# A tile of tokens takes one position of each quarter of 32 images, and x is loaded once

## The reference

```python
x = x + _L0_conv_ref(_gn(x), ...)      # group norm over (rows, columns, 2 channels), window attention + 3x3 convolution
t = _to_tokens(x)                      # (32, 256, 64)
t = t + _L1_attn_ref(_ln_t(t), ...)    # scores are sums over all 256 positions; softmax over the 32 images
t = t + _L1_ffn_ref(_ln_t(t), ...)     # top 2 of 8 experts, hidden size 682
return _from_tokens(t, x)
```

## Time and profile before

| what | us |
|---|---|
| median of 3 runs | 887.52 |
| profiled execution | 889.28 |
| its span | 887.4 |
| TensorE busy | 787.4 |
| VectorE busy | 623.4 |
| ScalarE busy | 436.9 |
| GpSimd busy | 395.0 |
| reload of x, median of its four DMAs from issue to landing | 7.7 |

### The profile page before, as it was taken

The page is one execution under the profiler, slowest core; times in us unless marked ns, Lnnn a source line. Parts: engine busy times, 40 slices in busy tenths (PEclk is TensorE's granted clock), DMA queues, the critical chain, the costliest instruction groups (busy, mean ns, idle before and its releaser), DMA issues.

```text
span 887.4 us, 22282 instructions
## 1 busy us (share of the span) xinstructions
PE 787.4 (89%) x7948; PEld 476.6 (54%) x7948; DVE 623.4 (70%) x1522; ACT 436.9 (49%) x828; POOL 395.0 (45%) x452
## 2 busy tenths in 40 slices
PE   4789999999978999799898879689989999999970
PEld 4757777777766565477777523223333333333450
DVE  6568898989845676367878667487756666666654
ACT  2536666666653344354453345345545555555540
POOL 1045555555531111004545565576666775444550
PEclk9969999999986999899997799699999999999985
DMA  6026310111009930000000410422052323231109
GB/s 213 1 45 120 48 22 13 21 26 26 2 5 343 338 108 2 2 1 18 19 18 21 69 35 21 69 48 46 25 82 48 62 50 53 41 49 32 26 7 284
DMA packets 180822, 54.55 MB, mean 61 GB/s; under 512 B 155936, under 2 KB 175361, under 8 KB 180464
## 3 DMA queue, kind: packets, MB, share of 16 engines
q1 hardware_dynamic: 167152, 43.35, 23.1%
q0 software_dynamic: 8704, 8.54, 2.9%
q10 hardware_dynamic: 4864, 1.31, 0.7%
HBM read 25.10 MB, written 28.51 MB: 60 GB/s over the span
## 4 chain that ended last, share of the span: by engine, by line
PE 36%; DVE 11%; issue 4%; POOL 3%; DMA 2%; ACT 1%; SPq 1%; ACTq 0%; POOLq 0%; DVEq 0%
PE bank L1344 17%; PE bank L1354 9%; PE bank L1282 2%; POOL slot_x L1222 2%; PE bank L1362 2%; DVE norm_T L1744 1%; PE bank L1273 1%; DMA slot_x<-rows,slots 1%; PE bank L1255 1%; POOL chosen_out L1233 1%; PE bank L1264 1%; PE bank L1291 1%; DVE av_og L1493 1%; ACT norm_T L1451 1%; DVE residual L1764 1%
## 5 line engine op out<-in xcount | busy, mean ns | idle before, releaser
L1344 PE MATMUL bank<-ex_xt,ex_w 64*128 64x512 f32 (+9 forms) x936 | 216.9, 588 | 24.0 <-DVE norm_T L1744 10.5
L1744 DVE TENSOR_TENSOR norm_T<-norm_T,bank 128x512 f32<-128x512 f32 (+7 forms) x234 | 141.9, 630 | 102.3 <-ACT norm_T L1451 99.3
L1233 POOL DMA_INDIRECT chosen_out<-ex_out,ex_id x144 | 143.3, 995 | 119.0 <-DVE norm_T L1744 45.1
L1451 ACT ACTIVATE norm_T<-bank 128x512 f32<-128x512 f32 (+7 forms) x234 | 129.7, 557 | 91.3 <-PE bank L1344 89.9
L1222 POOL DMA_INDIRECT slot_x<-rows,slots x128 | 124.6, 973 | 110.5 <-issue 63.9
L1344 PEld LDWEIGHTS bank<-ex_xt,ex_w 64*128 64x128 f32 (+1 forms) x936 | 79.6, 185 | 136.8 <-issue 102.6
L1354 PE MATMUL bank<-norm_T,ex_w 128*64 128x512 f32 (+7 forms) x468 | 103.5, 579 | 0.7 <-ACT ex_w L1438 0.7
L450 POOL TENSOR_TENSOR probs<-shifted,win_rden 128x512 f32<-128x512 f32 x64 | 66.7, 1042 | 14.1 <-DVE win_rden L622 8.2
L1354 PEld LDWEIGHTS bank<-norm_T,ex_w 128*64 128x64 f32 x468 | 30.7, 142 | 69.8 <-issue 53.1
L1444 ACT ACTIVATE norm_T<-bank 128x512 f32<-128x512 f32 (+7 forms) x39 | 21.8, 559 | 81.5 <-PE bank L1354 81.5
L442 POOL TENSOR_TENSOR xp<-norm_T,one_of_each 128x256 fp32r<-128x256 f32 x32 | 19.7, 615 | 83.2 <-PE ps_c L511 83.0
(11 more groups left out here) (263 smaller groups left out, 1380.9 us busy)
## 6 DMA issues: line engine op xcount, KB each, us to landing
slot_x<-blank SPq DMA_DIRECT2D x1, 17028.0 KB, 56.5
ex_x<-slot_x SPq DMA_DIRECT2D x128, 64.0 KB
norm_T<-chosen_out SPq DMA_DIRECT2D x8, 512.0 KB, 7.0
w_rows<-in_L_ffn_w_dram SPq DMA_DIRECT2D x32, 84.0 KB
wlocal_in<-in_L_conv_w_local_dram SPq DMA_DIRECT2D x6, 384.0 KB, 9.9
chosen_out<-ex_out,ex_id POOLq DMA_INDIRECT x144, 2.2
residual<-in_x_dram SPq DMA_DIRECT2D x2, 1024.0 KB, 7.2
residual<-in_x_dram SPq DMA_DIRECT2D x4, 512.0 KB, 7.7
```

The lines of the kernel that those rows point to most:

```text
L1233: eng.indirect_dma_start(s.chosen_out[:, :], bass.IndirectOffsetOnAxis(ex_id[k % OUTS][some, j:j + 1].bitcast(U32), 0), out[k % OUTS][some ...
L1344: eng.matmul(ps[b][0:units(c), 0:width(k)], w13[par][halves(i), c * HCHUNK:c * HCHUNK + units(c)], xt[par][halves(i), 0:width(k)], start=T ...
L1451: eng.activation(act[c % DEEP][0:units(c), 0:width(k)], ps_1[c % DEEP][0:units(c), 0:width(k)], ACT.Silu).then_inc(act_n, 1)
L1744: eng.tensor_tensor(h[par][0:units(c), c, 0:width(k)], act[c % DEEP][0:units(c), 0:width(k)], ps_3[c % deep3(k)][0:units(c), 0:width(k)], ...
```

## The change

A tile now holds position t of each quarter, t from 0 to 63: partition 32q+b, tile t is position 64q+t of image b. This is also the order in which the prologue can load x, so `s.x1` is loaded once and stays. The parts:

- x is loaded by eight DMAs (four quarters for each half), each to 32 partitions by 8 KB, and VectorE waits for four of them.
- The reload (L424 to L426), its semaphore and VectorE's wait are gone.
- `part_mean` has its ones at partitions 32 apart and is filled by seven `affine_select`, one for each diagonal, where two were.
- `turned_bank` reads PSUM with quarter and image exchanged.
- `evict` writes each image in four runs of 64 values, 512 B apart within a run.
- The stores write 32 partitions by one run of 2 KB.

```diff
-            return psA[...].rearrange("p k n -> p (k n)").rearrange("p (c b q) -> p b q c", c=WIN, q=QUARTER)
+            return psA[...].rearrange("p k n -> p (k n)").rearrange("p (c q b) -> p b q c", c=WIN, q=QUARTER)
...
-                src = a["x"].rearrange("b (q r) c e -> (b q) (r c) e", q=QUARTER)
+                src = a["x"].rearrange("b (q r) c e -> q b (r c) e", q=QUARTER)
                 for h in range(2):
                     some = slice(h * LHALF, (h + 1) * LHALF)
-                    eng.dma_start(x[:, some, :], src[:, some, :]).then_inc(x_in[h], 16)
+                    for q in range(QUARTER):
+                        eng.dma_start(x[q * BATCH:(q + 1) * BATCH, some, :], src[q][:, some, :]).then_inc(x_in[h], 16)
...
-                eng.memset(part_mean[:, :], 1.0 / (4 * QUARTER)).then_inc(filled, 1)
...
+                eng.memset(part_mean[:, :], 0.0).then_inc(filled, 1)
+                for q in range(1 - QUARTER, QUARTER):
+                    eng.wait_ge(filled, 1 + q + QUARTER)
+                    eng.affine_select(out=part_mean[:, :], in_=part_mean[:, :], compare_op=ALU.not_equal, fill=1.0 / (4 * QUARTER),
+                                      base=q * QP, pattern=[[-1, P]], channel_multiplier=1).then_inc(filled, 1)
...
-                    eng.wait_ge(x_in[h], 16)
+                    eng.wait_ge(x_in[h], 16 * QUARTER)
...
-                x = a["x"].rearrange("b (h4 r) c e -> b (h4 r c) e", r=1).rearrange("b (g q) e -> q b g e", q=4)
-                for q in range(4):
-                    eng.dma_start(s.x1[q * BATCH:(q + 1) * BATCH, :, :], x[q]).then_inc(s.x1_in, 16)
...
-                by_position = s.conv[:, :].rearrange("p (l b) -> p b l", b=BATCH)
+                by_position = s.conv[:, :].rearrange("p (t q b) -> p b q t", b=BATCH, q=QUARTER)
...
-                    eng.activation(by_position[:, n, :], onto_bank(n), ACT.Identity, ...)
+                    eng.activation(by_position[:, n], onto_bank(n).rearrange("p (q t) -> p q t", q=QUARTER), ACT.Identity, ...)
...
-                eng.wait_ge(s.x1_in, 16 * 4)
...
-        out_rows = out_dram.rearrange("b r c e -> b (r c) e").rearrange("b (g j) e -> j b g e", j=4)
+        out_rows = out_dram.rearrange("b r c e -> b (r c) e").rearrange("b (j g) e -> j b g e", j=4)
```

More of the change, by code:

```diff
@@ L88, in prologue @@
         x, twofold = s.x1, s.conv[:, :]
+        QP = P // QUARTER
         LHALF = L // QUARTER // 2
@@ L106, in prologue @@
         psG = own.enter_context(nc.psum_tensor("psG_w", [P, 512], F32))
-        ident_n, blocks_n, filled = sem("ident_done"), sem("part_mean_done"), sem("constants_filled")
+        ident_n, filled = sem("ident_done"), sem("constants_filled")
         loads, bias_in, local_in, x_in = sem("conv_w_loads"), sem("conv_bias_loads"), [sem(f"conv_local_in{i}") for i in range(3)], [sem(f"gn_x_in{h}") for h in range(2)]
@@ L124, in turned_bank @@
         def turned_bank(step):
-            return psA[:, step % 2 * 2:step % 2 * 2 + 2, :].rearrange("p k n -> p (k n)").rearrange("p (c b q) -> p b q c", c=WIN, q=QUARTER)
+            return psA[:, step % 2 * 2:step % 2 * 2 + 2, :].rearrange("p k n -> p (k n)").rearrange("p (c q b) -> p b q c", c=WIN, q=QUARTER)
         def home(step):
@@ L151, in _ @@
                                   base=0, pattern=[[-1, P]], channel_multiplier=1).then_inc(ident_n, 1)
-                eng.memset(part_mean[:, :], 1.0 / (4 * QUARTER)).then_inc(filled, 1)
[L153 to L158, removed]
+                eng.memset(part_mean[:, :], 0.0).then_inc(filled, 1)
[3 more added lines that the diff above has]
+                                      base=q * QP, pattern=[[-1, P]], channel_multiplier=1).then_inc(filled, 1)
                 eng.memset(s.fold[:, :], 0.0).then_inc(filled, 1)
                 for half in range(2):
-                    eng.wait_ge(filled, 4 + half)
+                    eng.wait_ge(filled, 2 * QUARTER + 2 + half)
                     eng.affine_select(out=s.fold[:, :], in_=s.fold[:, :], compare_op=ALU.not_equal, fill=1.0,
                                       base=-half * C, pattern=[[-1, C]], channel_multiplier=1).then_inc(filled, 1)
-                eng.wait_ge(filled, 6)
-                eng.wait_ge(blocks_n, 1)
+                eng.wait_ge(filled, 2 * QUARTER + 4)
                 eng.wait_ge(ident_n, 1)
@@ L209, in _ @@
                 last.then_inc(heads_done, 1)
-                eng.wait_ge(blocks_n, 1)
+                eng.wait_ge(filled, 2 * QUARTER + 1)
                 eng.wait_ge(sums_n, 1)
@@ L566, in exp @@
                     eng.activation(shifted[e][:, :, :], shifted[e][:, :, :], ACT.Exp).then_inc(exp_n, 1)
-                by_position = s.conv[:, :].rearrange("p (l b) -> p b l", b=BATCH)
+                by_position = s.conv[:, :].rearrange("p (t q b) -> p b q t", b=BATCH, q=QUARTER)
                 def evict(n):
                     eng.wait_ge(o_n, n + 1)
-                    eng.activation(by_position[:, n, :], onto_bank(n), ACT.Identity, bias=s.conv_bias[:, 0:1]).then_inc(evict_n, 1)
+                    eng.activation(by_position[:, n], onto_bank(n).rearrange("p (q t) -> p q t", q=QUARTER), ACT.Identity, bias=s.conv_bias[:, 0:1]).then_inc(evict_n, 1)
                 def body(n, par):
@@ L1788, in hybrid_block @@
                 s.xt = turned_x.enter_context(nc.sbuf_tensor("norm_T", [P, TOK], F32))
-                s.x1_in = sem("residual_in")
                 with ExitStack() as upto_scores:
```

## The result

The changed kernel takes 893.95 us (median of six runs, 891.53 to 896.41) against 888.36 for the kernel before (six runs, 886.62 to 889.70): ratio 1.0061, 95% interval 1.0039 to 1.0083. It is slower by 0.6%, some 5.5 us, and a second series of nine runs gave 1.0065 (1.0034 to 1.0095). The prediction was 888.8 and "the same", with 891.2 as its upper end. Its profiled execution took 891.97 us with a span of 890.2, 2.8 more than before; it is one of the shortest runs of the changed kernel, so the trace shows less than the loss.

What follows compares the result with a forecast made beforehand. It took the start to hang on x's landing and VectorE's statistics, the end on lagging 256 B stores. Load +3.4 and stores -2.1 gave +1.3 us on the 887.52 median: 888.8 us, range 885.2 to 891.2.

Steps and rivals of the forecast that it cites:

- The load of x: Start: eight DMAs to 32 partitions at about 207 GB/s delay VectorE's statistics by +3.4 us, between 0 and +4.8.
- 32 partitions cost nothing: Rival at the start: x still loads at 390 GB/s, only the end's gain remains, 885.4 us; chance 0.17.
- Weights late: Rival at the start: `wout_in` lands late and delays the `part_mean` matmul, +2.6 to +3.2 in all, 890.4 us; chance 0.15.
- `part_mean`, the turns and `evict`: Prologue and image evictions: 0 each; copies after the turns within 0.5 us either way, `evict` -0.3 to +0.7.
- The stores: End: 2 KB pieces keep the store queue empty at each part, so the span ends 2.1 us earlier, between -2.4 and 0.
- The reload and its wait: From 70 us on: removing them gains 0, as no engine noticed the reload and VectorE's wait comes after the last image.

Runs made afterwards that it cites:

- e1: Kernel before with x, in the old order, loaded by eight DMAs of 32 partitions: 891.81 us, ratio 1.0038.
- e10: Changed kernel with one x transfer per half (e7), and all stores held until the last expert rows landed: 917.97 us, ratio 1.0335.
- e13: Kernel before without the reload's four transfers, VectorE's wait kept on a load that landed long before: 887.30 us, ratio 0.9994.
- e9: Kernel before with the reload's four transfers cut to 8 KB each and the wait kept: 888.09 us, ratio 0.9982.
- e11: Changed kernel plus four 8 KB transfers that rewrite the same values, and VectorE's wait for them: 889.92 us, ratio 1.0012.
- e6: Changed kernel with the full reload of x and VectorE's wait put back: 892.27 us, ratio 1.0045.
- e15: Changed kernel with VectorE's wait alone put back, on a load that landed long before: 891.90 us, ratio 1.0039.
- e16: The two-queue kernel e12 with VectorE's wait put back: 893.22 us, ratio 1.0043.
- e12: Changed kernel with x on two queues, quarters 2 and 3 ahead of ScalarE's weights, convolution weights held until x landed: 891.61 us, ratio 1.0046.
- e7: Changed kernel with each half of x loaded by one transfer into all 128 partitions, in the new order: 914.42 us, ratio 1.0303.

## Why the prediction was wrong, point by point

- **The load of x: right.** +3.4 predicted, +3.16 in the trace; the series of e1 has 3.4, within 2 us either way. The choice between 390 and 207 GB/s fell on the right side: the narrow loads moved 202 to 238 GB/s with 8 KB pieces, in the new order and in the old (e1). The rival "32 partitions cost nothing" fell with it. The Trainium skill, page "SBUF — State Buffer", section "Door 1: The DMA port swizzle", has 189 GB/s for 32 partitions at 1 MiB and some 218 for long transfers; the rows lie about the second figure.
- **Weights late: did not happen.** In one trace `wout_in` landed at 13.52, 2.4 us later than before and short of the 14.3 from which it would have decided; in the five other traces with the same loads it landed earlier than before.
- **`part_mean`, the turns and `evict`: right, 0.**
- **The stores: the mechanism right, the size off.** -2.1 predicted, -1.2 in the trace; no series is fine enough to show it. The way from last sum to end shrank as forecast (5.3 to 3.4; 3.2 expected). What the term left out is that the quicker stores delay the last expert loads beside them: from the first load to the last sum it is 16.7 to 17.3 us in all 11 traces with 2 KB stores that are not held (all but e10's, with 16.1), and 15.9 to 16.2 in all eight with 256 B. I had written that VectorE's sums are what is late next and had not asked what feeds them.
- **The reload and its wait, 0: this is the step that failed.** In the kernel before, taking them away cost 0.31% and 0.36% in two series, 2.8 and 3.2 us, and keeping VectorE's wait alone (e13) brought it back to 0. With the start and the end of the trace that makes 4.7 to 5.2 us, against 5.4 and 5.8 by the two ratios, each with an interval of 2 us or more either way. The argument, that no engine noticed the reload, was true of its bytes (e9), and it was the wrong question: what goes away with a reload is also instructions. That this acts by the place of an engine's code relative to its fetches is argued from the traces, for 1.5 of these 3 us, and not shown. No row of before priced it. The trace of before did show TensorE's "issue" wait of 1.62 us under the 17 MB store, which I did not read.
- **The range failed with that step.** I took the spread of three runs, 2.8 us, for the blur. The same program spreads over 10 us in 35 runs, and a middle of 800 us, to which the change adds no work, still moved by 3.6. With start and end alone, +1.9, the time would have been some 890.3 and inside the range; e11, the change with 32 KB of idle loads, came to 889.92.

What stays open: why one waiting instruction of VectorE goes with TensorE's fetch at 22 instead of 27 us after the last image; where the other 1 to 2 us come from; and what in the middle of the changed kernel costs up to 4 us even with the wait (e6, e15, e16), when e11 is free of it.

## What to carry to other kernels

Cost a transfer into 32 partitions by a row of the same kernel with the same partitions, even when its pieces are of another size. When a store gets faster, ask which load runs beside it. Where a large background transfer fills the DMA engines, look for "issue" waits under it, and in a long kernel like this one give an edit that adds or removes instructions a few microseconds of uncertainty, however idle these instructions were. A control that keeps the instructions without their bytes tells the two apart. Before a small difference is explained, run each program twice: here one execution says little about 3 us in 890.

## What the runs showed of the hardware, unexpectedly

- Two queues, each loading 32 partitions at a time, moved 307 GB/s between 3 and 5 us and 260 between 5 and 9 (e12), where the changed kernel's one queue of x moved 222 and 238: 38% and 9% more. e12 also moves ScalarE's four weights behind x, so the gain is not of the queues alone. 1.9 us of the statistics' 3.2 came back. The Trainium skill, page "SBUF — State Buffer", section "Can I just issue two DMAs to hit both halves?", has 6% for two DMAs at partitions 0 and 64; here it is more.
- With a transfer whose source begins with a dimension of 4 the queues moved some 113 GB/s with 0.41 to 0.44 of the engines busy, at last 96 GB/s with 0.25, though it wrote all 128 partitions in 8 KB pieces (e7).
- Under the 17 MB store a code fetch of 16 KB starts 19 to 23 us or 26.6 to 27.1 us after the last image's eviction began, and the layers with the late one are 1.5 us longer in the mean (20 traces).
- TensorE is granted 0.5, its 1.2 GHz level, for 13.7 us around the first images in one trace of the kernel before and for 17.1 us in another, and the images behind them stand 1.1 us apart. The first trace of the changed kernel had 17.1 too, the second 13.7: of the 4.2 us by which its images were late in the first against the first trace of before, 1 us was this.
